# Constant matrix products on TensorE in two stretches of each stage, and the row numbers of the gather worked out on GpSimd

## The reference

```
x = x + gnn(adj, layernorm(x)):
    idx   = first S = 25 columns j with A[n, j] != 0
    agg   = max over idx of X[idx]            (max with 0 where degree <= S)
    out   = relu(concat(X, agg) @ W + b)
x = x + ffn(layernorm(x)):
    h = relu(x @ Wi.T + bi)
    twice: h = relu(h @ Ws.T + bs + h @ Wr[e].T + br[e] + h)     e = route of the tile
    out = h @ Wo.T + bo
```

## Time and profile before

| | us |
|---|---|
| median of 3 runs | 735.02 |
| lowest and highest | 734.71, 737.31 |
| the profiled execution | 736.18 |
| its span in the trace | 734.5 |

### The profile page before, as it was taken

One profiled execution on the slowest core, in us unless ns is written; L12 is line 12 of the kernel. 1 busy time (PEld: TensorE's weight loads), 2 busy tenths in 40 slices (PEclk: granted clock), 3 DMA queues, 4 the chain that ended last, 5 costly groups with the idle time before them and its releaser, 6 DMA issues.

```text
span 734.5 us, 11755 instructions
## 1 busy us (share of the span) xinstructions
PE 611.5 (83%) x3496; PEld 502.9 (68%) x3497; DVE 574.2 (78%) x959; ACT 521.2 (71%) x981; POOL 541.9 (74%) x388
## 2 busy tenths in 40 slices
PE   0466666679999799979997999899987999799686
PEld 0054545566987588858885888668875988588565
DVE  3766799878987898779987898789878987777740
ACT  5672455369977898779876987699769985478062
POOL 4577488497979987898878897989799878984000
PEclk9986798898999899979998999989998999799989
DMA  9999997479746965496638755785474543045222
GB/s 298 305 196 265 314 344 241 134 176 293 226 132 158 267 175 152 102 259 205 166 109 222 236 163 142 190 240 159 127 182 124 161 138 87 22 113 144 58 72 77
DMA packets 145171, 131.73 MB, mean 179 GB/s; under 512 B 72219, under 2 KB 112324, under 8 KB 145092
## 3 DMA queue, kind: packets, MB, share of 16 engines
q1 hardware_dynamic: 128124, 105.94, 53.5%
q0 software_dynamic: 7296, 15.74, 8.3%
q10 hardware_dynamic: 9680, 9.21, 4.5%
HBM read 98.20 MB, written 17.98 MB: 158 GB/s over the span
## 4 chain that ended last, share of the span: by engine, by line
PE 59%; DVE 22%; issue 5%; DVEq 4%; DMA 4%; ACT 4%; SPq 1%; ACTq 0%
PE slot_ps L777 28%; PE ffn_ps L842 11%; DVE acc L988 9%; PE ffn_ps L852 4%; PE ffn_ps L826 4%; PE prep_ps L869 3%; DMA at<-mask 2%; PE ffn_ps L811 2%; PE ffn_ps L792 2%; DVEq L1060 2%; DVE top L1047 2%; PE ffn_ps L812 2%; DMA adj_sb<-in_adj_dram 2%; DVE wst L1153 1%; DVE score L1049 1%
## 5 line engine op out<-in xcount | busy, mean ns | idle before, releaser
L777 PE MATMUL slot_ps<-onehot,xsplit 128*128 128x512 f32 (+3 forms) x1376 | 375.5, 401 | 51.1 <-DVE acc L988 44.4
L988 DVE TENSOR_TENSOR acc<-slot_ps,acc 128x896 f32<-128x896 f32 (+2 forms) x336 | 293.7, 884 | 77.3 <-PE slot_ps L777 74.5
L547 POOL TENSOR_SCALAR onehot<-rank,ranks 128x896 fp32r<-128x896 bf16 (+3 forms) x128 | 298.4, 2333 | 72.6 <-PE slot_ps L777 67.5
L777 PEld LDWEIGHTS slot_ps<-onehot,xsplit 128*128 128x128 f32 x1376 | 251.9, 204 | 105.7 <-issue 71.0
L535 POOL DMA_INDIRECT gath<-feature_table,idx x200 | 207.7, 1038 | 47.9 <-issue 42.6
L842 PE MATMUL ffn_ps<-hT,wst 128*128 128x128 f32 x1024 | 135.1, 277 | 0.0
L842 PEld LDWEIGHTS ffn_ps<-hT,wst 128*128 128x128 f32 x1024 | 129.0, 191 | 5.9 <-issue 0.8
L670 ACT ACTIVATE away<-rank,ranks 128x896 bf16<-128x896 bf16 (+4 forms) x136 | 107.9, 793 | 6.8 <-DVE wst L1153 6.4
L687 ACT ACTIVATE onehot<-away 128x896 fp32r<-128x896 bf16 (+4 forms) x136 | 96.3, 708 | 21.5 <-PE slot_ps L777 10.6
L629 ACT ACTIVATE hT<-ffn_ps,wst 128x128 f32<-128x128 f32 x256 | 81.1, 375 | 29.5 <-PE ffn_ps L842 27.3
L641 ACT ACTIVATE rank<-prep_ps 128x448 bf16<-128x448 f32 x128 | 63.0, 550 | 21.0 <-PE prep_ps L869 11.7
(11 more groups left out here) (121 smaller groups left out, 586.3 us busy)
## 6 DMA issues: line engine op xcount, KB each, us to landing
wst<-folded_weights SPq DMA_DIRECT2D x128, 257.0 KB, 2.9
adj_sb<-in_adj_dram SPq DMA_DIRECT2D x64, 512.0 KB, 5.9
folded_weights<-wst ACTq DMA_DIRECT2D x34, 256.0 KB, 6.9
hT<-in_L_ffn_Wr_dram SPq DMA_DIRECT2D x26, 256.0 KB, 10.3
xs<-in_x_dram SPq DMA_DIRECT2D x8, 512.0 KB, 8.1
feature_table<-xn SPq DMA_DIRECT2D x8, 512.0 KB, 4.1
x<-in_x_dram SPq DMA_DIRECT2D x8, 512.0 KB, 4.3
out_dram<-h SPq DMA_DIRECT2D x16, 256.0 KB, 2.4
```

What stands on the lines that cost most here:

```text
L547: pool.tensor_scalar(onehot[:, UNIT[n]:UNIT[n] + many, 0:wide * P], rank[:, b % 2, first:first + many, 0:wide * P], ranks[:, r - 1:r], Non ...
L777: mm = pe.matmul(slot_ps[n % 2][:, c0:c1], xsplit[:, b % 2, part, first + j, :], onehot[:, UNIT[n] + j, c0:c1], start=(j == 0 and part == ...
L988: dve.tensor_tensor(acc[:, p % 2, 0:cols], slot_ps[n % 2][:, 0:cols], acc[:, p % 2, 0:cols], ALU.max).then_inc(s_max, 1)
```

## The change

PE gets a new piece, `keep_busy`. In stages 2 to 8 it multiplies a constant tile by a constant tile ahead of the slots of positions 5 to 11: 2, 4, 5, 5, 4, 3 and 2 products of 128x128 by 128x512 in fp16, 25 a stage. In stage 9 it does 24, four at each of positions 6 to 11, behind `finish`. They write a PSUM buffer that the ranking uses later (`prep_f[0]`), and nothing reads them.

`rows_to_gather` moves from DVE (at position 28) to POOL (at position 30, in the first stage 17). Its three instructions become four, each waiting for the one before through the new semaphore `s_rows`. The gathers of the same stage begin at position 31 instead of 29, and some of the next stage move by one position; the order of DVE's maxima over the gathered rows stays.

```diff
-    GATHER_AT = {29: [0], 30: [1], 32: [2], 33: [3], 35: [4], 36: [5], 38: [6], 39: [7], 41: [8], 42: [9]}
+    ROWS_AT = [17, 30]
+    GATHER_AT = {31: [0], 32: [1], 33: [2], 35: [3], 36: [4], 37: [5], 39: [6], 40: [7], 42: [8], 43: [9]}
...
+    BUSY_AT = {5: 2, 6: 4, 7: 5, 8: 5, 9: 4, 10: 3, 11: 2}
+    BUSY_AT_END = {6: 4, 7: 4, 8: 4, 9: 4, 10: 4, 11: 4}
...
+            def rows_to_gather(s):
+
+                pool.wait_ge(s_top, TOPS * (s + 1))
+                if s >= 2:
+                    pool.wait_ge(s_hub, HUBS * (s - 1))
+                pool.tensor_scalar(spread[:, :], top[:, 0, 0:TOPK], 0.0, lane[:, 0:1], ALU.is_equal, ALU.mult
+                                   ).then_inc(s_rows, 1)
+                pool.tensor_scalar(floor[:, s % 2, 0:1], top[:, 0, TOPK:TOPK + 1], 0.0, NEG_BIG, ALU.is_gt, ALU.mult
+                                   ).then_inc(s_rows, 1)
+                pool.wait_ge(s_rows, 4 * s + 2)
+                pool.tensor_tensor(spread[:, :], spread[:, :], top[:, 0, 0:TOPK], ALU.subtract).then_inc(s_rows, 1)
+                pool.wait_ge(s_rows, 4 * s + 3)
+                pool.tensor_scalar(idx[:, s % 2, 0, :], spread[:, :], float(N), None, ALU.add).then_inc(s_rows, 1)
+                pool.wait_ge(s_rows, 4 * s + 4)
+
             def gather(b, j):
...
                 if j == 0:
-                    pool.wait_ge(s_idx, b + 1)
                     pool.wait_ge(s_tab[b % 2], 16 * (b // 2 + 1))
...
+                if s < B and p == ROWS_AT[s > 0]:
+                    rows_to_gather(s)
...
+            def keep_busy(s, p):
+
+                where = BUSY_AT if s < B + 1 else BUSY_AT_END
+                if p == min(where):
+                    pe.wait_ge(s_q, 2 * IT * min(s, B))
+                for _ in range(where.get(p, 0)):
+                    pe.matmul(prep_f[0][:, 0:BANK], down[:, 0:P], down[:, 0:BANK], start=True, stop=True)
...
+                    if s >= 2:
+                        keep_busy(s, p)
                     slot(s - 1, p)
                 if 2 <= s:
                     finish(s - 2, p)
+                if s == B + 1:
+                    keep_busy(s, p)
...
-                if p == TOP_AT[s > 0][-1] + 1:
-                    rows_to_gather(s)
...
+                if n == HUBS and s > 0:
+                    dve.wait_ge(s_rows, 4 * s)
...
-            def rows_to_gather(s):
-                h = 0
-                dve.wait_ge(s_top, TOPS * (s + 1))
-                if s >= 2:
-                    dve.wait_ge(s_hub, HUBS * (s - 1))
-                dve.tensor_scalar(spread[:, :], top[:, h, 0:TOPK], 0.0, lane[:, 0:1], ALU.is_equal, ALU.mult)
-                dve.tensor_scalar(floor[:, s % 2, h:h + 1], top[:, h, TOPK:TOPK + 1], 0.0, NEG_BIG,
-                                  ALU.is_gt, ALU.mult)
-                dve.drain()
-                dve.scalar_tensor_tensor(out=idx[:, s % 2, h, :], in0=spread[:, :], scalar=base[:, 0:1],
-                                         in1=top[:, h, 0:TOPK], op0=ALU.add, op1=ALU.subtract
-                                         ).then_inc(s_idx, 1)
...
                     larger(half_max[:, :], gath[:, 13, :], half_max[:, :]).then_inc(s_redB, 1)
+                    dve.wait_ge(s_rows, 4 * n)
```

More of the change, by code:

```diff
@@ L114, in gnn_ffn_program @@
     SPLIT_AT = 20
[L115 to L117 removed]
+    ROWS_AT = [17, 30]
+    GATHER_AT = {31: [0], 32: [1], 33: [2], 35: [3], 36: [4], 37: [5], 39: [6], 40: [7], 42: [8], 43: [9]}
+    GATHER_NEXT = {0: [10], 2: [11], 3: [12], 5: [13], 6: [14], 8: [15], 10: [16], 11: [17], 13: [18],
+                   15: [19], 16: [20], 18: [21], 20: [22], 21: [23], 23: [24]}
     GATHER_FIRST = {0: [0], 1: [1], 2: [2], 3: [3], 4: [4], 5: [5], 6: [6], 7: [7], 8: [8], 10: [9], 11: [10],
@@ L272, in gnn_ffn_program @@
         s_six = sem("s_six")
+        s_rows = sem("s_rows")
         s_redB = sem("s_redB")
```

3 lines of the change are left out of this document (removed).

## The result

The changed kernel takes 755.18 us, median of 4 runs (754.22 to 756.7), against 736.12 for the kernel before on the same chip. The ratio is 1.0262, 95% interval 1.0231 to 1.0292: slower by 19 us. The forecast of 735.0 us and its range of 727 to 741 missed it.

What follows compares the result with a forecast made beforehand. It took the chain to lie mostly on PE (59%) and DVE (22%), changing hands within a stage. Terms 11.2 - 2.6 - 2.9 - 4.0 - 1.6 = +0.1 us on the profiled 736.18, carried to the median: 735.0 us, range 727 to 741.

Steps and rivals of the forecast that it cites:

- The constants ahead of slots 5 to 7: Eleven products on PE's chain make slot 7's maximum 1.6 us later in each of seven stages: +11.2 us.
- 11.2 - 2.6 - 2.9 - 1.6: Constants' delay in seven stages, less full-clock gains in six middle stages, in stage 8 and in the last stage.
- what the clock gives back: PE stays at full clock behind the constants: -2.6 us over six middle stages and -2.9 us in stage 8.
- The fourteen ahead of slots 8 to 11 at nothing: These constants, 3.0 us a stage, fall where PE waits for DVE anyhow, so they cost nothing.
- rival 4: The clock falls all the same behind slot 10, so the 2.6 and 2.9 us don't come: 740.5 us, chance 0.18.
- the forecast's 0.43: Mean worth in us of a full PE clock per middle stage, between 0.86 in stage 5 and nothing in stage 6.
- the floor of 7.83: Stage 6's time in us from the end of `shift` to the first `wiT` product, taken as ACT's own work.
- The 2.9 us of stage 8: Gain from full clock at slots 12 to 14 and two groups of transposes, where half clock costs PE in full.
- The row numbers: Moved off DVE, they end PE's 0.67 us wait at slot 29 in stages 2 to 7: -4.0 us.
- POOL's own work at nothing: POOL is 0.7 to 2.6 us later at slot 43's one-hot; its 2.66 us wait there hides that: 0.
- The last stage: Constants fill PE's 6.19 us wait ahead of position 12's transposes; transposes and `wiT` products run at full clock: -1.6 us.
- Rival 5: POOL's four instructions and waits take over 3.3 us, past its 2.66 us of room: 741 us, chance 0.05.

Runs made afterwards that it cites:

- const_only: All constants alone added to the kernel before, with row numbers on DVE and gathers at their old positions: 745.5 us, ratio 1.012.
- const_8_to_11: Only the 14 constants a stage ahead of slots 8 to 11 added to the kernel before, none in the last stage: 736.4 us, ratio 1.000.
- const_late: Kernel before plus 22 constants a stage ahead of slots 10, 11 and 12, where PE waited, and those of the last stage: 734.4 us, ratio 0.997.
- all_oldtab: The whole change with both gather tables as before it: 738.2 us, ratio 1.004 to the kernel before.
- rows_three: The change without constants, with gather 5 moved from position 37 to 39: 741.6 us, ratio 1.008 to the kernel before.

## Why the prediction was wrong

- **The constants ahead of slots 5 to 7** were right. 0.217 us apiece was forecast and 0.218 measured; slot 7's maximum at 15.4 was forecast and 15.35 measured. All constants together cost 9 us on the kernel before (const_only), against +4.1 by the forecast's terms (11.2 - 2.6 - 2.9 - 1.6): it is what the clock gives back that was too large, in stage 8 and the last stage above all.
- **The fourteen ahead of slots 8 to 11 at nothing**: right in sum (const_8_to_11, ratio 1.000).
- **The clock** was half right. It fell in five of six middle stages all the same, which was rival 4, but for 3.4 to 6.8 us in place of 6.8 to 10.2. Where it was held (const_late), the worth in a middle stage was 0.29 us against the forecast's 0.43. From the end of `shift` to the first product with `wiT` the kernel after needs 7.87 us in stage 5 (411.70 to 419.57), near the floor of 7.83 that the forecast read from stage 6, and 7.8 to 8.5 in the six; with the clock held all six stand at that floor, so it was read rightly. The 2.9 us of stage 8 were oversized: 0.4 us with the clock held.
- **The row numbers** were right in place: the maximum of slot 29 no longer waits for DVE's row numbers, and the stage gains 0.9 us there, by slot 31. Against the kernel before, with the old tables, it is worth 1.3 us in all and not 4.0: the stretch up to slot 12 grows by some 0.4 us a stage in the profile, presumably by POOL's other moments, which no run shows by itself. The prediction took the 2.25 us of `spread` for DVE's own work. For the most part they were a wait for POOL's one-hot, the same kind of meeting that then made the loss; the sign of it was that POOL needs 0.41 us for the same instruction (447.54 above). POOL's own work at nothing was right: the four instructions and their waits take 1.3 us and the wait behind the gathers hides them.
- **The last stage**: -1.2 us in the profile after against -1.6. That was luck: five of the seven profiles with these constants took 0.3 to 0.5 us more than the kernel before there.
- **The step that failed** is "Against that goes POOL's wait for `idx` [...] with as many gathers in front as before [...] That wait hides it: 0". It costs POOL's side of the change by POOL's own lateness alone. The two new tables, in which all ten gathers of the first and six of fifteen of the second moved, got no term, no bound and no rival. The runs put 16 us there (all_oldtab against the whole change, 738.2 and 755.2). The two ways were a reduction on DVE that met POOL's one-hot at its start (1.15 us a stage) and PE's signals held behind a fourth gather in a row (1.05 us a stage). They make 2.2 of the 2.5 us by which a middle stage is longer than in all_oldtab; the other 0.3 lie ahead of slot 26 and are not assigned. Rival 5, POOL late, has the right engine and the wrong mechanism: POOL was on time and in the way.

With the tables left as they were the sum would have been off by 3 us. Part of that is luck too: apart, the constants cost 5 us more than the forecast's terms for them and the row numbers brought 2.7 us less, which would make 8.

## What to carry to other kernels

When a table moves an engine's work, don't only ask whether that engine is late. Lay its new times beside those of the engine that it excludes, and look where an instruction of the one now starts within a few tenths of a microsecond of the other's; a shift of one position was worth 1 us a stage here, in either direction. A row that is far longer than its work (2.25 us for 128x25) may be a wait, and can tell which engines exclude each other before anything is changed. Filler work costs nothing only where its engine waits in the trace, and is worth only what the engine behind it doesn't already bound. When parts of a change are timed apart and don't add up, look for a meeting in time, since it is the phase that each part moves.

## What the runs showed of the hardware

- DVE's and POOL's work exclude each other, but not for every pair of operations and moments. DVE's one-hot of 128x1792 took from 1.14 to 4.24 us by how it met POOL, and its 128x25 `spread` 2.25 and 1.18 us, each time up to 0.04 us behind the end of POOL's one-hots. A 128x384 reduction of two tensors took 0.55 us in the middle of a POOL one-hot and 1.46 us when it started 0.03 us ahead of one. The Trainium skill, SBUF — State Buffer, section SBUF: two separate sides, says that whichever starts first keeps the pair for the whole instruction and the other fully blocks, and names a DVE operation with two SBUF inputs against a GpSimd operation that reads SBUF as such a pair. The reduction is one, and doesn't fit that: neither order gave a full block of 2.5 us.
- With four indirect transfers issued in a row by POOL, PE's signals came in a burst 1.9 us after the start of the fourth, though PE's products went on. It made slot 37 late in all middle stages of the three kernels in which slot 37 ended before that moment, and in none with three in a row. Why a fourth does it was not found. That breaking the row removes it is shown by three kernels (rows_three and the two with two entries altered), all with the same gather moved to the same place.
- A full-clock product of 512 fp16 columns costs 0.218 us of PE's chain in a run of equal ones.
